# Moving the state kernel of a convolution from one stage's GpSimd time to two earlier stages

## The reference, cut to what matters

```
dt = jnp.exp(log_dt)
A = A_re + 1j * A_im
C = C_re + 1j * C_im
dtA = dt[:, None] * A
dC = C * (jnp.exp(dtA) - 1.0) / A
powers = jnp.exp(dtA[:, :, None] * jnp.arange(L))
K = 2.0 * jnp.einsum('dn,dnl->dl', dC, powers).real
...
y = jnp.fft.irfft(xf * Kf.T[None], n=n, axis=1)[:, :L]
return y + x * D_skip
```

## Time and profile before

| | |
|---|---|
| Median of 3 runs | 632.76 us |
| The runs | 632.33, 632.76, 637.3 us |
| Profiled execution, first to last instruction (its span) | 630.7 us |
| Median less that span | 2.06 us |
| Busy share of the span: TensorE, VectorE, ScalarE, GpSimd | 87%, 69%, 48%, 21% |
| TensorE's mean granted clock, of 2.4 GHz | 0.956 |

### The profile page before, as it was taken

The page is one execution under the profiler, slowest core; times in us unless marked ns, Lnnn a source line. Parts: engine busy times, 40 slices in busy tenths (PEclk is TensorE's granted clock), DMA queues, the critical chain, the costliest instruction groups (busy, mean ns, idle before and its releaser), DMA issues.

```text
span 630.7 us, 12259 instructions
## 1 busy us (share of the span) xinstructions
PE 550.6 (87%) x5014; PEld 339.2 (54%) x5015; DVE 433.5 (69%) x841; ACT 300.7 (48%) x372; POOL 133.2 (21%) x199
## 2 busy tenths in 40 slices
PE   8999998998799999879994594599889879999988
PEld 4755665676355566434452264294557435556656
DVE  6845326756967865666999999936556696786144
ACT  2868881425657687102664560022112255768711
POOL 3212001000000000205798899500100000000000
PEclk9999998899999999999998588699789999999999
DMA  8645481573200000001022045034300160000000
GB/s 216 152 125 147 121 340 42 169 200 81 100 3 1 2 2 3 2 0 53 0 93 112 1 153 115 20 77 103 133 1 2 37 263 1 3 3 2 2 0 3
DMA packets 17258, 45.47 MB, mean 72 GB/s; under 512 B 4153, under 2 KB 13226, under 8 KB 16362
## 3 DMA queue, kind: packets, MB, share of 16 engines
q1 hardware_dynamic: 17076, 44.47, 23.5%
q0 software_dynamic: 128, 0.23, 0.1%
HBM read 34.28 MB, written 8.29 MB: 68 GB/s over the span
## 4 chain that ended last, share of the span: by engine, by line
PE 53%; DVE 34%; ACT 4%; issue 4%; POOL 3%; SPq 1%; DMA 0%; DVEq 0%; ACTq 0%; POOLq 0%
PE psum L1471 9%; DVE values L3317 9%; PE psum L1457 8%; DVE l2x_best L3309 7%; PE psum L318 4%; PE psum L1446 4%; PE psum L856 3%; PE psum L1967 3%; PE psum L865 3%; PE psum L3167 2%; POOL rstd L260 2%; PE psum L453 2%; PE psum L3134 2%; DVE ring L1619 2%; PE psum L1994 2%
## 5 line engine op out<-in xcount | busy, mean ns | idle before, releaser
L260 POOL TENSOR_TENSOR rstd<-rstd,minus_half 64x1 f32<-64x1 f32 x20 | 11.9, 594 | 400.5 <-DVE rstd L268 400.5
L318 PE MATMUL psum<-ones 128*128 128x512 f32 (+3 forms) x188 | 75.8, 521 | 0.3 <-ACT experts L1210 0.3
L1567 ACT ACTIVATE ring<-psum,l3x_gain_columns 128x1024 f32<-128x1024 f32 x49 | 54.3, 1113 | 23.6 <-PE psum L1457 23.6
L1567 ACT ACTIVATE ring<-psum,l1x_gain_columns 128x1024 f32<-128x1024 f32 x49 | 54.3, 1113 | 22.3 <-PE psum L1457 22.3
L1471 PE MATMUL psum<-ring,values 128*32 128x128 f32 x1568 | 62.7, 279 | 0.4 <-ACT ring L1567 0.4
L972 ACT ACTIVATE ring<-psum,l0x_key_scale 128x1024 f32<-128x1024 f32 x49 | 52.1, 1113 | 5.7 <-PE psum L856 5.7
L1471 PEld LDWEIGHTS psum<-ring,values 128*32 128x32 f32 x1568 | 37.0, 109 | 28.1 <-issue 24.7
L318 PEld LDWEIGHTS psum<-ones 128*128 128x128 f32 x188 | 32.2, 192 | 27.9 <-issue 25.8
L1672 DVE TENSOR_REDUCE l1x_tops<-psum 128x1 f32<-128x448 f32 x64 | 36.7, 618 | 10.2 <-PE psum L1446 10.1
L1672 DVE TENSOR_REDUCE l3x_tops<-psum 128x1 f32<-128x448 f32 x64 | 36.7, 618 | 10.2 <-PE psum L1446 10.1
L3309 DVE MAX8 l2x_best<-values 128x8 f32<-128x6272 f32 x6 | 40.1, 6691 | 0.1
(11 more groups left out here) (776 smaller groups left out, 1071.6 us busy)
## 6 DMA issues: line engine op xcount, KB each, us to landing
wide<-keys_aside SPq DMA_DIRECT2D x54, 224.0 KB, 3.8
experts<-in_experts SPq DMA_DIRECT2D x1, 4608.0 KB, 13.7
experts<-in_experts SPq DMA_DIRECT2D x1, 4096.0 KB, 15.0
keys_aside<-ring SPq DMA_DIRECT2D x7, 448.0 KB, 2.5
keys_aside<-experts SPq DMA_DIRECT2D x6, 448.0 KB, 3.2
ring<-in_ctx_tiles SPq DMA_DIRECT2D x1, 2352.0 KB, 9.0
experts<-in_experts SPq DMA_DIRECT2D x1, 2048.0 KB, 7.9
ctx_t<-in_ctx_t SPq DMA_DIRECT2D x3, 672.0 KB, 7.6
```

What stands on the lines that cost most here:

```text
L318: mem.nc.tensor.matmul(mem.psum[:, bank, 0:n * 128], mem.ones[:, :], spread(mem.ones[:, :], 1, [128, n, 128]), start=True, stop=True)
L1567: nc.scalar.activation(probs[:, t % PROBS, :].rearrange("p (b n) -> p b n", b=2), ps[:, pair:pair + 2, :], ACT.Exp, scale=exp_gain[:, :]). ...
```

## The change

The state kernel is made in two parts, both on GpSimd and both earlier. `pool_angles` (down to the event `angles`) stands in the first expert stage, behind its norm. `pool_kernel` (the rest) stands in the second attention, behind its norm; ahead of the first lag it waits for the key transfers out of `experts` and for the events `Q_stack` of ScalarE and VectorE. The sine is ScalarE's first instruction in the second attention. Its arrays lie in `experts` behind the first expert weights and, once those are used, over them, and one product buffer in `ring`; `LAGS` is 8. ScalarE waits for the finished kernel ahead of the copies of the quantised weights, which go into the same columns; the convolution's wait stays. The five weight arrays move from the pack `l2x` to `l0f`. The arithmetic is the same, operation by operation.

```
-    "l0f": [("w_router", C, E), ("b1", C, E * HID // C), ("b2", E, C)],
+    "l0f": [("w_router", C, E), ("b1", C, E * HID // C), ("b2", E, C), ("log_dt", C, 1), ("A_re", C, NSTATE),
+            ("A_im", C, NSTATE), ("C_re", C, NSTATE), ("C_im", C, NSTATE)],
...
# stage_long_attention
-    pool_done.stage("rstd")
+    pool_done.stage("rstd", *(["state_kernel"] if level == 1 else []))
...
             @block.scalar
...
+                if level == 1:
+                    mem.state_kernel.act(act)
                 for n in late_keys:
                     high(n)
...
             @block.gpsimd
             def _(pool):
                 pool_rstd(mem, "var", "rstd")
+                if level == 1:
+                    mem.state_kernel.pool_kernel(pool, [
+                        (stacked, 16 * PER_STACK), act_done.at("Q_stack"), dve_done.at("Q_stack")])
...
# stage_topk_experts
+    if level == 0:
+        mem.state_kernel = StateKernel(mem)
...
                 pool_rstd(mem, "var", "rstd")
+                if level == 0:
+                    mem.state_kernel.pool_angles(pool)
...
# stage_rope_attention
             @block.scalar
             def _(act):
+                act.wait_ge(*mem.state_kernel.ready)
                 mem.quantised.act(act, WEIGHT_BANKS)
                 heads.act(act)
...
# StateKernel
-    LAGS = 16
-    COLUMNS = (T + T // 2 + 2 * LAGS) * NSTATE
+    LAGS = 8
+    SPARE, LATER = 2 * E * HID, (2 * LAGS + T + T // 2) * NSTATE
...
+        self.prod1 = lags(mem.ring, PROBS_COLUMNS, self.LAGS)
+        self.prod2 = lags(mem.experts, 0, self.LAGS)
+        self.qi = lags(mem.experts, self.LAGS * N, T // 2)
+        self.qr = lags(mem.experts, (self.LAGS + T // 2) * N, T)
...
+    def pool_kernel(self, pool, lags_free):
...
+        pool.wait_ge(*self.angles_ready)
+        self.exponential(re, grow, grow_m1, N)
         pool.wait_ge(*mem.act_done.at("sines"))
...
+        for event in lags_free:
+            pool.wait_ge(*event)
         sub(qr[:, 0, :], t1, t2)
...
# stage_topk_attention
-                state_kernel.act(act)
                 aside.act(act)
...
                 pool_rstd(mem, "a_var", "a_rstd")
-                state_kernel.pool(pool)
                 pool_rstd(mem, "x_mid_var", "h_rstd")
...
-                dve.wait_ge(*pool_done.at("state_kernel"))
+                dve.wait_ge(*mem.state_kernel.ready)
```

More of the change, by code:

```diff
@@ L2087, in stage_topk_experts @@
     act_done.stage("exp")
-    pool_done.stage("rstd")
+    pool_done.stage("rstd", *(["angles"] if level == 0 else []))
+    if level == 0:
+        mem.state_kernel = StateKernel(mem)
     weights = mem.experts
@@ new lines, with __init__, columns, lags @@
+    SPARE, LATER = 2 * E * HID, (2 * LAGS + T + T // 2) * NSTATE
+    def __init__(self, mem):
+        N = NSTATE
+        self.mem = mem
+        at = count(self.SPARE, N)
+        def columns(n=N):
+            first = [next(at) for _ in range(-(-n // N))][0]
+            return mem.experts[:, first:first + n]
+        self.wide = {n: columns() for n in ["re", "im", "turns", "t1", "t2"]}
+        self.angles, self.sines = (columns(2 * N).rearrange("p (m n) -> p m n", m=2) for _ in range(2))
+        few = columns()
+        self.dt, self.dt_m1, self.log_dt, *scratch = (few[:, n:n + 1] for n in range(7))
+        self.scratch = {1: (*scratch[0:3], scratch[3].bitcast(I32))}
+        at = count(self.LATER, N)
+        self.wide |= {n: columns() for n in ["grow", "grow_m1", "cos", "cos_m1", "nr", "gr", "gi", "size"]}
+        self.pr, self.pi = (columns(2 * N).rearrange("p (m n) -> p m n", m=2) for _ in range(2))
+        self.scratch[N] = (columns(), columns(), columns(), columns().bitcast(I32))
+        def lags(of, first, n):
+            return of[:, first:first + n * N].rearrange("p (l n) -> p l n", n=N)
+        self.prod1 = lags(mem.ring, PROBS_COLUMNS, self.LAGS)
+        self.prod2 = lags(mem.experts, 0, self.LAGS)
+        self.qi = lags(mem.experts, self.LAGS * N, T // 2)
+        self.qr = lags(mem.experts, (self.LAGS + T // 2) * N, T)
@@ new lines, in w, with mul, add, sub @@
+    def w(self, name):
+        return self.mem.w("l0f", name)
+    def mul(self, out, a, b):
+        self.mem.pool_step(self.mem.nc.gpsimd.tensor_tensor(out, a, b, ALU.mult))
+    def add(self, out, a, b):
+        self.mem.pool_step(self.mem.nc.gpsimd.tensor_tensor(out, a, b, ALU.add))
+    def sub(self, out, a, b):
+        self.mem.pool_step(self.mem.nc.gpsimd.tensor_tensor(out, a, b, ALU.subtract))
+    def affine(self, out, a, scale, shift):
+        self.mem.pool_step(self.mem.nc.gpsimd.tensor_scalar(out, a, scale, shift, ALU.mult, ALU.add))
@@ new lines, in exponential @@
+    def exponential(self, z, full, less_one, n):
+        p, step, mul, add = self.mem.nc.gpsimd, self.mem.pool_step, self.mul, self.add
+        whole, rest, series, power = self.scratch[n]
+        step(p.tensor_scalar(z, z, -87.0, 88.0, ALU.max, ALU.min))
+        self.affine(whole, z, LOG2E, ROUND)
+        step(p.tensor_scalar(whole, whole, ROUND, None, ALU.subtract))
+        step(p.tensor_scalar(series, whole, -LN2_HI, None, ALU.mult))
+        add(rest, series, z)
+        step(p.tensor_scalar(series, whole, -LN2_LO, None, ALU.mult))
+        add(rest, series, rest)
+        step(p.tensor_scalar(series, rest, 1.0 / 5040, None, ALU.mult))
+        for k in (720, 120, 24, 6, 2, 1):
+            step(p.tensor_scalar(series, series, 1.0 / k, None, ALU.add))
+            mul(series, series, rest)
+        step(p.tensor_scalar(power, whole, 127.0, 8388608.0, ALU.add, ALU.mult))
+        two = power.bitcast(F32)
+        mul(series, series, two)
+        add(full, series, two)
+        step(p.tensor_scalar(less_one, two, -1.0, None, ALU.add))
+        add(less_one, less_one, series)
@@ L2937, in pool @@
+        re, im, turns, t2 = (self.wide[n] for n in ["re", "im", "turns", "t2"])
+        dt, angles = self.dt, self.angles
+        pool.wait_ge(mem.loaded["l0f"], 16)
+        step(p.tensor_copy(self.log_dt, w("log_dt")))
+        self.exponential(self.log_dt, dt, self.dt_m1, 1)
         step(p.tensor_scalar(re, w("A_re"), dt, None, ALU.mult))
@@ L2947, in pool, with pool_kernel @@
             .then_inc(*mem.pool_done.mark("angles"))
-        exponential(re, grow, grow_m1, N)
+        self.angles_ready = mem.pool_done.at("angles")
+    def pool_kernel(self, pool, lags_free):
+        mem, w, mul, add, sub = self.mem, self.w, self.mul, self.add, self.sub
+        p, step = mem.nc.gpsimd, mem.pool_step
+        N = NSTATE
+        re, t1, t2, grow, grow_m1, cos, cos_m1, nr, gr, gi, size = (
+            self.wide[n] for n in ["re", "t1", "t2", "grow", "grow_m1", "cos", "cos_m1", "nr", "gr", "gi", "size"])
+        sines, pr, pi, qr, qi = self.sines, self.pr, self.pi, self.qr, self.qi
+        pool.wait_ge(*self.angles_ready)
+        self.exponential(re, grow, grow_m1, N)
         pool.wait_ge(*mem.act_done.at("sines"))
```

101 lines of the change are left out of this document (28 added, 73 removed).

## The result

Four runs of each kernel gave a median of 645.0 us after (641.68 to 650.14) against 633.5 before (632.33 to 637.3). The ratio is 1.0177, with a 95% interval of 1.0115 to 1.0238. The profiled execution is the slowest of the four: 650.14 us, span 648.4, so 17.7 us more than the span of before.

The account below looks back on a forecast made before the run. VectorE was taken to set the top-k stage's pace, GpSimd having 24 us to spare; terms 0.5 + 0.4 + 1.2 + 3.3 + 1.0 = +6.4 on the 630.7 span gave 637.1, plus 2.06 made 639 us, range 632.5 to 646.

Parts of the forecast that it names:

- 1: Rival at the second attention's chunk ends: GpSimd yields and VectorE loses nothing; 0 to +5 us, most likely 633.5; chance 0.24.
- 2: Rival: only products with two SBUF inputs meet GpSimd, not the scalar operation and cast between them; 636.8 us; chance 0.14.
- 3: Rival at the folds: GpSimd's 10.59 us power holds the port throughout, a fold waits some 9 us; 648 us; chance 0.10.
- 4: Rival: GpSimd slows the top-k stage, its going gives back 1.5 us; 631.3 us; chance 0.06, shared with unknown gains.
- Start +0.5: Second attention's start: the norms, eight copies and similar VectorE operations are stretched by GpSimd; +0.5 us (0 to 1.3).
- folds +0.4: Five VectorE folds of 1.08 us: the first one or two meet short GpSimd instructions, the others a harmless power; +0.4 us.
- A raised top beside products of 512: +3.3: Chunk end in the second attention: small VectorE operations wait for GpSimd products; +3.3 us each (1.1 to 4.7).
- two to four products; I take three: Raised top: one or two small operations pass per GpSimd product, so four operations need three; 2.6 us of the wait.
- a seam, +1.2: First chunk end, near 205.7 us: falls near a gap between GpSimd's phases of 512; +1.2 us (0.5 to 4.7).
- The second top, +3.3: Second chunk end, near 230 us: falls in GpSimd's third phase of products of 512; +3.3 us.
- I reckon that GpSimd loses about 6 us: Second attention: GpSimd loses about 6 us to VectorE at start and folds, which places its later phases and tree.
- The tail, +1.0 (0 to 3): Rounding of quantised weights beside GpSimd's tree of sums: some 4 us of waiting, less 3.2 to spare; +1.0 us.

Follow-up runs that it names:

- power_product: Kernel before, with a GpSimd power of 128x64 started ahead of the first raised top and a product of 128x2048 ahead of the second; 638.53 us, ratio 1.0083.
- gated: Changed kernel, with GpSimd waiting ahead of certain products until the first and the second raised top are cast; 642.66 us, ratio 1.0146.
- before_delayed: Kernel before, with five VectorE memsets of 128x512 ahead of each of two raised tops in the second attention; 646.05 us, ratio 1.0196.
- delayed_filled: Kernel before, with five VectorE memsets ahead of each raised top and sixteen unread matmuls on TensorE while it waits; 640.33 us, ratio 1.0117.
- the second profile: Profile of the changed kernel run again with no edit; 643.6 us median, ratio 1.0125.
- used_later: Changed kernel, with the addition that makes `used` moved behind the two casts that release the scores; 645.14 us, ratio 1.0172.
- before_filled: Kernel before, with TensorE's filling matmuls ahead of the first turn of the time-mixing stage lengthened from 256 to 896 columns; 632.06 us, ratio 0.9978.

## Why the prediction was right or wrong

**The place and the mechanism were right.** The time is lost at the raised tops of the second attention, where small VectorE operations wait for the end of GpSimd's instruction; the fourth attention is unchanged; folds beside the power stay at 1.08 to 1.09; GpSimd and ScalarE are late for nobody; the top-k stage gives nothing back. Four rivals fall: 1, since VectorE does wait; 2, since the cast (1.13) and the scalar rounding (4.80) wait as well as the products; 3, by the folds beside the power and by power_product; 4, since the top-k stage takes 133.76 us from its first search for a maximum to the first product of the convolution (312.40 to 446.16), against 133.49 before (294.00 to 427.49). One reading of the prediction was too simple: the norm's row does not quite agree with the rule that whichever engine starts first has the port, since that norm began at 445.34, 0.08 ahead of GpSimd's memset of 0.79, and was held all the same; only a memset of 0.10 had begun before it, at 445.26.

**The direction was right, the size was not.** 639.0 us was forecast and "within 1%" given 0.57; the ratio is 1.8% over, and 645.0 lies near the upper end of 646. Term by term:
- Start +0.5 and folds +0.4: measured 0 (norm +2.07, first fold at 163.72 or +2.05). The eight copies took 2.18 us instead of 1.82, but VectorE waits for ScalarE behind them, 1.71 us instead of 2.20, so nothing of it reached the folds; the folds lie beside the power.
- A raised top beside products of 512: +3.3 forecast, 2.69 in the first profile, 1.61 and 2.80 in the second. The step "two to four products; I take three" was too dear for the four operations: two to three waits in all, since every second operation slips in ahead of the next product. At the first end "a seam, +1.2" was not met.
- The second top, +3.3 forecast, cost 5.71 in the first profile and 2.80 in the second. In the first the tree's first addition of 2048 elements lay on it, which the sum had on the rounding. Two things brought them together. The step "I reckon that GpSimd loses about 6 us" failed: it needed 250.5 - 145.6 = 104.9 us from the norm on, against my 247.4 - 143.56 = 103.8 undisturbed, so that in both profiles the tree came some 5 us sooner behind the norm than I had it. And in the first profile the second top came later: 1.54 us were lost between the norm and the first top, 2.69 at that top and 3.07 behind it. In the second, where only 1.61 us were lost, the tree came too late for the top. So whether the two meet hangs on what the clock takes in an execution, which no step of the sum had.
- The tail, +1.0 (0 to 3): none in the first profile, but where the tree did meet the rounding (gated) it cost 7.38 - 1.16 = 6.2. The step "some 4 us of waiting" took the tree as one wait; its first three additions each held an operation up (4.80, 2.57 and 1.89 us).
- Left out altogether: the granted clock behind a stalled top, 3.07 and 3.30 us in the first profile, as much again as a raised top, and 0 and 1.01 in the second. before_delayed shows it without GpSimd and delayed_filled shows it gone. The sum had stall times only, and a stall of TensorE was priced at its own length.

The sum for the first profile, 8.4 + 6.4, leaves 3.6 us ahead of the first top, which gated, with the same work up to that top and +0.21 there, does not put down to the change. That profile is of the slowest execution. The forecast had 1.2 + 3.3 = 4.5 us at the two tops; the first profile has 8.4 there, with the tree on the second top, and the second profile 4.41. The waits of the first alone would have given 632.8 + 8.4 = 641, those of the second 637. That 645.0 still lies in the range is in part luck: the sum left out the clock, which took 6.4 us behind the casts in one profile and 1.0 in the other.

**Why nothing was to be won.** The state kernel had 24 us to spare where it was. Moved, it meets a stage in which a small VectorE operation stands on the path at the tops, ahead of the saved sums and in the rounding, one after the other. used_later and gated each cleared one of the places and got the wait at the next.

## What to carry to other kernels

Before work goes onto an idle GpSimd, look at what VectorE does beside it: reductions from PSUM and folds beside a power lost nothing here, while every small SBUF operation on the path could lose up to the whole length of a GpSimd product or sum, so the longest such instruction sets the price of a wait, and cutting it cut that price. Count a stall of TensorE at more than its length: here delays of 1.6 to 5.7 us at a top were followed by 0 to 4.4 us more, with the granted clock between 0.62 and 1.00, and by none when TensorE was kept busy. And a wait taken from one operation must be followed to whatever stands behind it in the engine's order.

## What the runs showed of the hardware that was not expected

- GpSimd's power of 128x64 (10.55 us) held up none of the VectorE operations of the raised top beside it; its product of 128x2048 (4.51 us) held a 128x8 operation, so that it took 3.89 us instead of 0.17.
- GpSimd is hardly slowed in return: 104.9 us for a count of 103.8, with products of 512 at 1.26 to 1.30 us throughout the stage.
- TensorE's clock does not always fall behind the same idle time. Early in the program TensorE stands idle for 1.21 us in before (up to 32.09) and in the changed kernel (up to 32.60); from 30 to 37 us the granted clock was 1.00 in the one and 0.76 in the other. Times of one kernel lie in steps: before_delayed gave 643.6 to 644.2 three times, at a mean granted clock of 0.946, and 647.9 to 648.2 three times, at 0.938 to 0.941. In before_filled one fall was taken away, and another came where before has none.
